# Routed experts with places from a ranking by weight: one block of 196 rows an expert, inner weights stationary, against two tiles of 128 rows

## The reference, as far as it matters

```python
logits = flat @ Wr
probs = jax.nn.softmax(logits, axis=-1)
topk_p, topk_i = jax.lax.top_k(probs, TOP_K)                 # 2 of 8 experts
...
capacity = max(1, math.ceil(n * TOP_K / NUM_EXPERTS * CAPACITY_FACTOR))   # 196
score = jnp.where(assigned, w_tok, -jnp.inf)
order = jnp.argsort(-score, axis=1)[:, :capacity]
dispatch = flat[order]
gate = jax.nn.silu(jnp.einsum('ech,ehi->eci', dispatch, w1))  # 768 x 192
up = jnp.einsum('ech,ehi->eci', dispatch, w3)
expert_out = jnp.einsum('eci,eih->ech', gate * up, w2)        # 192 x 768
expert_out = expert_out * weight_sel[..., None]
```

## Time and profile before

| what | value |
|---|---|
| median of 3 runs | 1425.91 us (1425.64 to 1432.25) |
| the profiled execution's own time | 1427.06 us |
| its span, first to last instruction | 1425.2 us |
| TensorE busy, mean granted clock | 1304.8 us (92%), 0.951 |
| VectorE busy | 972.3 us (68%) |
| ScalarE, POOL busy | 566.5 us (40%), 649.6 us (46%) |

### The profile page before, as it was taken

How to read it: one execution, slowest core, us unless ns; L and a number is a source line. 1 busy time by engine, 2 the same in 40 slices (tenths; PEclk the granted TensorE clock), 3 DMA queues, 4 the chain that set the end, 5 groups by cost and what they waited for, 6 DMA issues and landing times.

```text
span 1425.2 us, 22697 instructions
## 1 busy us (share of the span) xinstructions
PE 1304.8 (92%) x7467; PEld 1097.5 (77%) x7467; DVE 972.3 (68%) x2084; ACT 566.5 (40%) x670; POOL 649.6 (46%) x569
## 2 busy tenths in 40 slices
PE   7988578899999979999999999999999879989993
PEld 5765578556996869999999999999867569656661
DVE  8967898878689655565656565666159865367655
ACT  0010576232433044545554555454148651213330
POOL 7025777777666533354435434443268720111103
PEclk9999687999999989999999999999999979989997
DMA  7970000020740337787878787877589853427646
GB/s 174 89 134 6 2 2 1 2 67 2 207 105 2 102 140 278 267 271 282 273 282 278 274 276 283 283 272 265 137 264 320 273 166 91 133 80 233 200 131 199
DMA packets 112837, 243.87 MB, mean 171 GB/s; under 512 B 30574, under 2 KB 52266, under 8 KB 112668
## 3 DMA queue, kind: packets, MB, share of 16 engines
q1 hardware_dynamic: 76252, 131.74, 31.6%
q0 software_dynamic: 22432, 72.27, 17.8%
q10 hardware_dynamic: 14080, 38.93, 7.3%
HBM read 202.05 MB, written 45.31 MB: 174 GB/s over the span
## 4 chain that ended last, share of the span: by engine, by line
PE 69%; DVE 19%; issue 4%; DMA 3%; ACT 2%; POOL 1%; DVEq 0%; SPq 0%; ACTq 0%; POOLq 0%; another core or an unknown queue 0%
PE PS L2807 29%; PE PS L2683 4%; PE PS L3014 4%; PE PS L2472 4%; PE PS L2797 3%; PE PS L2940 3%; PE PS L2621 3%; PE PS L2870 3%; PE PS L3025 3%; PE PS L2758 3%; DVE e L1379 2%; PE PS L2982 2%; DVE e L1621 2%; DVE e L1658 2%; DVE mlo L2221 2%
## 5 line engine op out<-in xcount | busy, mean ns | idle before, releaser
L854 POOL DMA_INDIRECT xg<-xn_dram,xrow x70 | 116.1, 1659 | 277.5 <-DVEq L1588 247.4
L2807 PE MATMUL PS<-whi,xhi 128*128 128x384 f32 x840 | 221.1, 344 | 1.0 <-ACTq L1167 1.0
L2807 PE MATMUL PS<-whi,xlo 128*128 128x384 f32 x840 | 215.0, 337 | 0.0
L2807 PE MATMUL PS<-wlo,xhi 128*128 128x384 f32 x840 | 213.7, 335 | 0.0
L1379 DVE TENSOR_TENSOR wlo<-raw,whi 128x2304 fp32r<-128x2304 f32 x68 | 175.3, 2578 | 37.4 <-ACTq L1150 30.9
L1148 ACT ACTIVATE whi<-raw 128x2304 fp32r<-128x2304 f32 x68 | 145.1, 2133 | 21.5 <-PE PS L2779 6.4
L1379 DVE TENSOR_TENSOR xlo<-PS,xhi 128x768 fp32r<-128x768 f32 x70 | 67.1, 958 | 125.2 <-ACTq L1159 118.3
L2807 PEld LDWEIGHTS PS<-wlo,xhi 128*128 128x128 f32 x840 | 152.3, 188 | 0.0
L2807 PEld LDWEIGHTS PS<-whi,xlo 128*128 128x128 f32 x840 | 152.1, 188 | 0.0
L2807 PEld LDWEIGHTS PS<-whi,xhi 128*128 128x128 f32 x840 | 148.6, 189 | 1.3 <-issue 1.3
L822 POOL DMA_INDIRECT evwb<-inv_dram,idxb x80 | 108.3, 1353 | 30.6 <-issue 22.4
(11 more groups left out here) (481 smaller groups left out, 2676.6 us busy)
## 6 DMA issues: line engine op xcount, KB each, us to landing
raw<-in_L_gnn_W_rel SPq DMA_DIRECT2D x68, 1152.0 KB
z_dram<-xn ACTq DMA_DIRECT2D x70, 384.0 KB, 7.4
wroot<-in_L_ffn_w SPq DMA_DIRECT2D x12, 576.0 KB, 6.7
y_dram<-yb ACTq DMA_DIRECT2D x17, 384.0 KB, 4.3
pre<-in_L_ffn_w SPq DMA_DIRECT2D x9, 576.0 KB, 4.8
gw<-in_L_gnn_W SPq DMA_DIRECT2D x2, 2304.0 KB, 27.1
fw<-in_L_ffn_w SPq DMA_DIRECT2D x8, 576.0 KB
fw<-in_L_ffn_w ACTq DMA_DIRECT2D x1, 4608.0 KB
```

What stands on the lines that cost most here:

```text
L854: pool.indirect_dma_start(xg[b][j][:, :], None, xn_dram, bass.IndirectOffsetOnAxis(ap=xrow[:, b, j:j + 1], axis=0)).then_inc(x_gathered[b] ...
L2807: mm = pe.matmul(slot(q)[:, s * BANK:s * BANK + HALF], a[:, k, :], wt[:, k, s * HALF:(s + 1) * HALF], start=(k == 0 and part == 0), stop=( ...
```

## The change

The place of a row in its expert's list is now its rank by weight: ranking comes first, `places` goes, and nobody beyond 196 is in a list. An expert is one block of 196 rows (`CAP`), gathered and turned in two halves of 98 (`HT`). In the inner product the weights are stationary, in three blocks of 128 columns (gate 0 to 127; gate and up 128 to 191 together; up 0 to 127), and the 196 turned rows stream, so that the hidden values come out turned and the turn by TensorE goes. The outer product is made twice, for 98 rows each. The further tile, the loops and tables for more and the filling of y_dram go. The ranking counts larger-or-equal scores in earlier groups, larger ones in its own and later groups, and equal ones of earlier rows within its own group. `ROUTE_JOBS` is TensorE's order of score rows and lists. Weights are loaded in three and two transfers instead of two and one.

```diff
 SH = T
-MORE_OF = NE
-ITEMS = ([(None, t) for t in range(SH)] + [(e, j) for e in range(NE - 1) for j in range(RT)] + [(MORE_OF, 0)]
-         + [(NE - 1, j) for j in range(RT)])
-OWN = SH + NE * RT + 1
...
-        SLOT3["rank", (_n - RANKS_FROM) // 2] = len(SLOT3)
+HT = CAP // 2
 RING = 3
-FIRST2 = (NE - 1) * RT * 128
-MANY2 = 4 * -(-2 * N * MORE // (4 * ((RT + MORE - 1) * 128 + 1)))
-LAST2 = FIRST2 + MANY2 * 128
...
+RANKED_AHEAD = 3
+SPREAD_AHEAD = 4
+ROUTE_JOBS = [("row", 0), ("row", 1), ("list", 0), ("row", 2), ("list", 1), ("row", 3)]
+for _n in range(NE):
+    ROUTE_JOBS += [job for job in (("list", _n + RANKED_AHEAD - 1), ("row", _n + SPREAD_AHEAD)) if job[1] < NE]
+assert CAP % 2 == 0 and len(ROUTE_JOBS) == 2 * NE
+INNER = {"gate": (0, 0), "up": (1, CAP), "both": (1, 0)}
...
-            fxT = [sb(f"fxT{b}", [128, K, 128], f32, g) for b in range(2)]
-            gate = [tail[:, b * F:(b + 1) * F] for b in range(2)]
+            fxT = [sb(f"fxT{b}", [128, K, CAP], f32, g) for b in range(2)]
+            gate = [tail[:, b * 2 * CAP:(b + 1) * 2 * CAP].rearrange("p (c n) -> p c n", c=2) for b in range(2)]
+            hidden = [sb(f"hidden{b}", [128, 2, CAP], f32, g) for b in range(2)]
...
-            earlier = sb("earlier", [P, T, N], f32, g)
+            earlier = sb("earlier", [P, P], f32, g)
...
             def load_w13(e, b, signal):
-                for n in range(2):
-                    sp.dma_start(w13[b][:, :, n * F:(n + 1) * F], v13[n][e]).then_inc(signal, 16)
+                for first, n, of in ((0, 0, slice(0, F)), (F, 1, slice(128, F)), (256, 1, slice(0, 128))):
+                    sp.dma_start(w13[b][:, :, first:first + of.stop - of.start], v13[n][e, :, :, of]).then_inc(signal, 16)
+
+            def load_w2e(e, b):
+                sp.dma_start(w2e[b][:, 0, :], v2[e][0:128, :]).then_inc(ld_w2e[b], 16)
+                sp.dma_start(w2e[b][0:F - 128, 1, :], v2[e][128:F, :]).then_inc(ld_w2e[b], 16)
...
-            for n in range(NE * RT + 1):
-                e, j = ITEMS[SH + n]
-                if j == 0:
-                    pool.wait_ge(rows2_ready, e + 1)
-                if n >= 4:
-                    pool.wait_ge(turned, n - 3)
-                b = n % 4
-                pool.indirect_dma_start(fx[b][:, :], None, xn_dram,
-                                        bass.IndirectOffsetOnAxis(ap=xrow2[:, e, j:j + 1], axis=0)).then_inc(x_gathered[b // 2][b % 2], 16)
-
-            def further_gather2(m):
...
+            for e in range(NE):
+                pool.wait_ge(rows2_ready, e + 1)
+                for j in range(RT):
+                    k = e * RT + j
+                    if k >= 4:
+                        pool.wait_ge(turned, k - 3)
+                    b = k % 4
+                    pool.indirect_dma_start(fx[b][0:HT, :], None, xn_dram,
+                                            bass.IndirectOffsetOnAxis(ap=xrow2[0:HT, e, j:j + 1], axis=0)).then_inc(x_gathered[b // 2][b % 2], 16)
...
-            pool.wait_ge(y_begun, 16 * (MANY2 // 4))
             for b in range(2):
-                pool.wait_ge(y_stored[b], 16 * ((NE - 1) * RT // 2 + (b == 0)))
+                pool.wait_ge(y_stored[b], 16 * (NE - 1))
...
-            def y_out(n):
-                k = n - SH
-                act.wait_ge(outer_full, n + 1)
-                if k >= 2:
-                    act.wait_ge(y_stored[k % 2], 16 * (k // 2))
...
+            def expert_gates(n):
+                act.wait_ge(inner_full, SH + 3 * n + 1)
+                step.do(act.activation(gate[n % 2][:, 0, :], slot(1)[:, 0:CAP], ACT.Silu))
+                act.sem_inc(gate_ready, 1)
+                act.wait_ge(inner_full, SH + 3 * n + 3)
+                step.do(act.activation(gate[n % 2][0:F - 128, 1, :], slot(1)[0:F - 128, BANK:BANK + CAP], ACT.Silu))
+                act.sem_inc(gate_ready, 1)
...
+            for j in range(RT):
+                take_x(0, j)
+            score_row(3)
+            for n in range(NE):
+                expert_gates(n)
+                if n + 1 < NE:
+                    take_x(n + 1, 0)
+                y_out(n, 0)
+                if n + 1 < NE:
+                    take_x(n + 1, 1)
+                if n + SPREAD_AHEAD < NE:
+                    score_row(n + SPREAD_AHEAD)
+                y_out(n, 1)
...
+            def rank(e, first, end):
+
+                row = srow[e % 2]
+                if first == 0:
+                    dve.wait_ge(srow_ready, e + 1)
+                for i in range(first, end):
+                    own = scol[e % 2][:, i:i + 1]
+                    if i:
+                        do(dve.tensor_scalar(compared[:, 0:i, :], row[:, 0:i, :], own, None, ALU.is_ge, ALU.add, accum_out=level[:, i, e:e + 1]))
+                    do(dve.tensor_scalar(compared[:, i:T, :], row[:, i:T, :], own, None, ALU.is_gt, ALU.add, accum_out=above[:, i, e:e + 1]))
+                    do(dve.scalar_tensor_tensor(compared[:, i, :], row[:, i, :], own, earlier[:, :], ALU.is_equal, ALU.mult,
+                                                accum_out=tied[:, i, e:e + 1]))
+
+            def placed(e):
+
+                r, chosen = picked[:, 0, :], picked[:, 1, :]
+                do(tt(r, above[:, :, e], level[:, :, e], ALU.add))
+                do(tt(above[:, :, e], r, tied[:, :, e], ALU.add))
+                do(dve.scalar_tensor_tensor(chosen, above[:, :, e], float(CAP), asg[:, :, e], ALU.is_lt, ALU.mult))
+                do(dve.scalar_tensor_tensor(place[:, :, e], above[:, :, e], 1.0, chosen, ALU.add, ALU.mult))
+                do(ts(poscol[:, :], place[:, :, e], -1.0, None, ALU.add))
+                if e + 2 < NE:
+                    column2(e + 2)
                 for t in range(T):
-                    step(dve.tensor_scalar(inlist2[e % 4][:, t, :], iota16[:, 0:RT * 128], place[:, t, e:e + 1], None, ALU.is_equal))
+                    step(dve.tensor_scalar(inlist2[e % 4][:, t, 0:CAP], iota16[:, 0:CAP], poscol[:, t:t + 1], None, ALU.is_equal))
                 step.sync()
                 dve.sem_inc(inlist2_ready, 1)
 
             def rows2(e):
-                dve.wait_ge(full[3], BEFORE["slot3"][3] + SLOT3["lists", e // 2] + 1)
-                L = slot(3)[:, e % 2 * 2 * RT:(e % 2 + 1) * 2 * RT].rearrange("p (j c) -> p j c", c=2)
-                do(dve.tensor_copy(node[:, :], L[:, :, 0]))
-                do(dve.scalar_tensor_tensor(xrow2[:, e, :], L[:, :, 1], 128.0, node[:, :], ALU.mult, ALU.add))
-                if e % 2 == 1:
-                    free_slot(3)
...
+            def expert_hidden(n):
+                dve.wait_ge(gate_ready, SH + 2 * n + 2)
+                step(tt(hidden[n % 2][:, 0, :], gate[n % 2][:, 0, :], slot(1)[:, BANK + CAP:BANK + 2 * CAP], ALU.mult))
+                do(tt(hidden[n % 2][0:F - 128, 1, :], gate[n % 2][0:F - 128, 1, :], slot(1)[F - 128:128, BANK:BANK + CAP], ALU.mult))
+                dve.sem_inc(h2_ready, 1)
...
                 dve.sem_inc(yrow_ready, 1)
-
-            def rank(e, part):
-
-                row = srow[e % 2][:, :, :]
-                if part == 0:
-                    dve.wait_ge(srow_ready, e + 1)
-                for i in range(T):
-                    own = scol[e % 2][:, i:i + 1]
-                    if part == 0:
-                        do(dve.tensor_scalar(compared[:, :, :], row, own, None, ALU.is_gt, ALU.add, accum_out=small[:, 8, i, e:e + 1]))
-                    else:
-                        do(dve.scalar_tensor_tensor(compared[:, :, :], row, own, earlier[:, i, :].rearrange("p (t c) -> p t c", c=P),
-                                                    ALU.is_equal, ALU.mult, accum_out=small[:, 9, i, e:e + 1]))
...
+                column2(e)
+            do(dve.memset(level[:, 0, :], 0.0))
+            add_shared(0)
+            dve.wait_ge(earlier_ready, 1)
+            rank(0, 0, 2)
             add_shared(1)
-            for e in range(2):
-                rows2(e)
+            rank(0, 2, 4)
...
+            rank(0, 4, T)
+            placed(0)
...
+            rows2(0)
+            rank(1, 0, 2)
...
-            further_upto = further_tables()
-            for k in range(2):
-                column2(k)
-            dve.wait_ge(earlier_ready, 1)
-            for n in range(SH, OWN):
-                if n in LISTS_AT:
-                    pair = LISTS_AT.index(n)
-                    for e in (2 * pair, 2 * pair + 1):
-                        rows2(e)
-                dve.wait_ge(gate_ready, n + 1)
-                do(tt(hh[n % 2][:, :], gate[n % 2][:, :], slot(1)[:, F:2 * F], ALU.mult))
-                dve.sem_inc(h2_ready, 1)
...
+            rank(1, 2, T)
+            placed(1)
+            rows2(1)
+            rank(2, 0, 3)
+            for n in range(NE):
+                expert_hidden(n)
+                if n == 0:
+                    rank(2, 3, T)
+                    placed(2)
+                if n + RANKED_AHEAD - 1 < NE:
+                    rows2(n + RANKED_AHEAD - 1)
```

(70 more changed lines are left out.)

424 lines of the change are left out of this document (75 added, 349 removed).

## The result

The changed kernel takes 1430.91 us (median of 19 runs, 1426.33 to 1434.79), the kernel before, run beside it, 1424.85 (19 runs, 1419.82 to 1433.43): ratio 1.0039, with an interval of 1.0021 to 1.0057. It is slower by 6.1 us between the medians (5.6 by the ratio); 6.0 faster was forecast. The profiled execution's own time is 1432.78 us at a span of 1431.2.

What follows compares the result with a forecast made beforehand. TensorE led the old chain (69%), with VectorE becoming a second bound. Loop 19.2 us gained, start 14.2 lost and tail 1.0 gained gave -6.0, from 1425.91 to 1419.9; range 1408 to 1433, likeliest case 1414 to 1425.

Steps and rivals of the forecast that it cites:

- the tail: After the last outer product: lower gathers begin earlier ahead of the last store, worth 0 to some 2 us, taken as 1.0.
- The start's length: Routing's end to inner product 0: 25.9 us of VectorE work plus waits; inner product 0 starts at 1280.8, 14.2 later than before.
- The inner product: TensorE, each expert: 36 passes of 0.165 us, together 5.94, against 7.74 for two old tiles.
- rival B: Inner product: weight loads set the pace at 190 ns; +6.2 us, 1426; chance 10%.
- E: Inner product of 196 columns costs what two 128-row tiles did, 7.74 instead of 5.94; 14.4 more, 1434; chance 2%.
- The ranking: VectorE, each expert: 14 instructions, 7.55 us; 1.56 a group of 125 rows, 1.30 for the first.
- VectorE's period: Expert loop: VectorE, ranking queued behind its wait for the list, takes 14.6 us a period, above TensorE's 14.5.
- Outer: two times 2.58: TensorE, each expert: two outer products of 2.58 us, since 384 columns still stream; 98 rows save nothing.
- I take 3.5 and 3: Start: clock-loss allowance, after 3.4 us lost in the old start; without any, the start is 3.7 shorter.
- Hidden 0 begins 6.6 after inner product 0: Expert 0: first hidden values begin 6.6 us after inner product 0 starts, at 1287.4.
- Rival C: Start: runs longer at half clock, or lists queue worse; +7.4 us, 1427; chance 12%.
- D: Expert loop: clock falls behind TensorE's waits, 3.4 us a fall; four reach +7.6, one an expert 1447; chance 12%.

Runs made afterwards that it cites:

- the seven profiles: The changed kernel's two profiles and five from follow-ups leaving its start unchanged; inner product 0 takes 7.04 to 7.06 or 8.39 to 8.55 us.
- experiment 3: Changed kernel with the second half of each outer product contracting 128 rows, 64 of them zeros, instead of 64; ratio 0.9999 to the kernel before.
- run 7: Changed kernel with list job before the first outer product from expert 1 on, and outer products contracting 128 rows twice; ratio 0.9964 to the kernel before.
- run 2: Changed kernel with the list job moved before the first outer product from expert 1 on; ratio 1.0004 to the kernel before.
- run 10: On top of run 7, products that compute nothing in TensorE's waits at the start and before list 2; 144.6 us from routing to last outer product.
- pair of second profiles: Changed kernel and kernel before, each profiled once more unedited; 162.1 and 152.8 us from routing to the last outer product.
- runs 1 and 5: Changed kernel plus, in 1, products computing nothing in start waits, ratio 1.0037; in 5, last ranking group of experts 3 to 7 done twice, stage 167.7 us.
- run 4: Changed kernel with gate and both parts of expert 0's inner product issued before list 1 and row 3; ratio 1.0032 to the kernel before.
- the early list: Edit placing the list job before the first outer product from expert 1 on; alone on the changed kernel, ratio 1.0004 to the kernel before.

## Why the prediction was wrong

The last outer product was forecast 147.2 after routing and came at 160.9, 13.7 later; the tail gave back more than forecast. Of the 13.7, 6.3 is the clock, in steps that the prediction had priced at full clock; 3.9 is the change between 128 and 64 rows, which it did not have; 3.5 stands, as far as durations tell, in the first products behind waits, priced as if TensorE never paused. Step by step:

| step | forecast | measured | more |
|---|---|---|---|
| inner product 0 starts (us after routing) | 31.1 | 31.1 | 0.0 |
| to hidden 0 | 6.6 | 8.9 | 2.3 |
| period of expert 0 | 16.9 | 20.4 | 3.5 |
| experts 1 and 2 | 14.6, 14.6 | 15.6, 15.6 | 2.0 |
| expert 3 | 14.5 | 17.3 | 2.8 |
| expert 4 | 14.4 | 15.3 | 0.9 |
| experts 5 and 6 | 13.7, 13.7 | 14.5, 14.4 | 1.5 |
| hidden 7 to the end | 7.1 | 7.8 | 0.7 |

**What held.** The start's length came out to 0.1 us, from 25.9 us of VectorE and the waits. Luck has a part in it: in the seven profiles with this start, inner product 0 begins 31.1 to 32.6 after routing, and the profile compared has the lowest value. The inner product: at full clock 6.18 with the change of rows before it and 5.98 without, against 5.94, so 0.165 a pass; the loads set no pace, and the recorded 190 ns misleads (it is 190 ns after the change as well, with passes of 0.166 to 0.172; rival B falls, E too). The ranking: the first group 1.29 us, then 1.56 a group (1312 to 1325 in VectorE's timeline; the list follows at 1324.68). VectorE's period: where it bounds, in experiment 3, it is 14.9 to 15.3, forecast 14.6. The loads of weights are hidden.

**What failed first: the price of an outer product and of what follows it.** "Outer: two times 2.58, since 384 columns still stream; the 98 rows save nothing" took the old row's duration for another operand. I looked at the columns and at the rows of the output and not at the contraction, which changed from 96 and 96 to 128 and 64. Experiment 3 gives its price: 0.17 in each outer product and 0.15 to 0.20 in what follows, 0.7 an expert in the chain and 0.5 in the periods of the experts without jobs. The remainder of a steady expert's 1.1 stands in the first products behind TensorE's waits: its first outer product takes 2.82 even with full rows, the score row 0.81 for 0.55, the list 0.43 for 0.3. Together with what is like it in the other experts this is 7.4 of the 13.7 (the table's right column less the clock's part, below). Of the 7.4, the rows are 3.9, measured by run 7 against run 2; the other 3.5 is read from durations, and no run takes it out.

**Second: the clock.** "I take 3.5 and 3" for the start stopped short of inner product 0, and the working behind it costed "Hidden 0 begins 6.6 after inner product 0" and the whole first period at full clock. Rival C had named TensorE's idle 1268 to 1278, and it is what came: 2.3 in inner product 0, 0.6 in row 4 and 1.65 in outer product (0, 1), 4.5 in all. D came once, 1.7 in expert 3 (its row 1.41 and outer product 3.82 for 0.81 and 2.75). Together 6.3. How much falls on the start varies by execution (inner product 0 takes 7.04 to 8.55 in the seven profiles, against 6.14 in run 10). Experiment 10 takes 5.5 out by giving TensorE work that nobody needs. The range held the result because the rivals were priced; the sign was missed since hand-over prices and clock erred the same way, which I had given no chance of its own.

**Third: the tail**, forecast at -1.0, is -2.5 (20.5 for 23.0) and -1.0 in the pair of second profiles (21.7 for 22.8), so the size was right within what it varies. The last store lands in 2.63 and the gather starts 3.4 after its issue, where it took 5.3 before (3.4 and 4.2 in the second pair). That fits the cause given, the lower gathers in the queues; no run tests it. A slip of reading beside it: the old end, 1399.35 + 2.58, should be 1402.2, since the row has 2.85.

**The structure** was right where it mattered for the repair: VectorE "stands at the list: outer product, turn and list lie ahead of it on TensorE, and the ranking is queued behind that wait". I counted that as a cost of the change without asking whether the order of the jobs could be otherwise; moved by one place, it is worth 4.5 in the loop (run 2).

Not tried: the 17th tile alone, since its removal is tied up with the tables for further tiles in the kernel before. Open: why the clock falls in the loop of the changed kernel at the same place in both profiles, in other places of runs 1 and 5, not at all in run 4, which has the same loop, and in none with the early list. In experiment 3 the loop kept the clock at 1.00 too, with TensorE busy 13.34 of 15 us from 1322 to 1337, about the share that the changed kernel had ahead of its fall (14.29 of 16 from 1326 to 1342); no row here explains the difference.

## What to carry to other kernels

Where a matmul keeps its columns but changes its contraction, ask whether neighbours on TensorE now differ in the number of rows; padding a half of 64 rows with zeros to 128 can be cheaper than the change back and forth. Cost the first products behind a stretch in which TensorE waits at the lower clock, up to where the trace shows that it comes back; if the waits can't be removed, products that compute nothing may pay (here 5.5 us): they need not hold the clock, it is enough that it is back when the real work starts. And when an engine both waits for a small result and has long work queued behind that wait, move the small job into a wait that is there already before shortening the long work.
